# The lower mixture layer of a perceiver block: factor gather spread over the token steps, in eight half tiles

## What is computed

```python
def kmoe(x_flat, W_router, A, B, scale, bias, d_in1, d_in2, d_out1, d_out2, top_k):
    logits = x_flat @ W_router.T
    vals, idx = jax.lax.top_k(logits, top_k)          # 2 of 64 experts
    probs = jax.nn.softmax(vals, axis=-1)
    xs = x_flat.reshape(-1, d_in1, d_in2)
    Y = jnp.einsum('nkoi,nij,nkpj->nkop', A[idx], xs, B[idx])
    out = jnp.einsum('nkop,nk->nop', Y, probs).reshape(-1, d_out1 * d_out2)
    return out * scale + bias
```

## Time and profile before

| | us |
|---|---|
| median of 3 runs | 1326.34 (1323.18 to 1327.03) |
| profiled execution, time | 1326.24 |
| profiled execution, span of its trace | 1324.2 |
| TensorE busy (matmul) | 1235.5, 93% |
| VectorE busy | 809.8, 61% |
| ScalarE busy | 439.6, 33% |
| GpSimd busy | 227.7, 17% |

### The profile page before, as it was taken

One profiled execution on the slowest core, in us unless ns is written; L12 is line 12 of the kernel. 1 busy time (PEld: TensorE's weight loads), 2 busy tenths in 40 slices (PEclk: granted clock), 3 DMA queues, 4 the chain that ended last, 5 costly groups with the idle time before them and its releaser, 6 DMA issues.

```text
span 1324.2 us, 61286 instructions
## 1 busy us (share of the span) xinstructions
PE 1235.5 (93%) x27823; PEld 799.4 (60%) x27823; DVE 809.8 (61%) x1523; ACT 439.6 (33%) x866; POOL 227.7 (17%) x373
## 2 busy tenths in 40 slices
PE   9999999999999999999999998887889888889885
PEld 6764333333333334677666775666777776779775
DVE  5567767776777671455565555555674846465766
ACT  2223211321132112221222211235464646454564
...
DMA packets 68176, 211.50 MB, mean 160 GB/s; under 512 B 14544, under 2 KB 30928, under 8 KB 53616
## 3 DMA queue, kind: packets, MB, share of 16 engines
...
...
## 4 chain that ended last, share of the span: by engine, by line
PE 77%; DVE 10%; issue 5%; DMA 3%; POOL 2%; ACT 2%; SPq 1%; DVEq 0%; POOLq 0%; ACTq 0%
PE ps L715 14%; PE ps L564 10%; PE ps L1088 8%; PE ps L2192 6%; PE ps L2143 4%; PE ps L235 4%; PE ps L1202 4%; PE ps L1109 4%; DVE arena L576 4%; PE ps L479 3%; PE ps L2121 2%; PE ps L2234 2%; PE ps L705 2%; DVE arena L1872 2%; PE ps L2178 2%
## 5 line engine op out<-in xcount | busy, mean ns | idle before, releaser
L576 DVE STREAM_TRANSPOSE arena<-arena 128x448 f32<-128x448 f32 (+1 forms) x512 | 264.0, 578 | 100.8 <-PE ps L564 83.8
L564 PE MATMUL ps<-arena 32*64 32x400 f32 (+1 forms) x4096 | 202.7, 506 | 0.8
L715 PE MATMUL ps<-arena 128*64 128x512 f32 x832 | 189.1, 598 | 0.0
L564 PEld LDWEIGHTS ps<-arena 32*64 32x64 f32 x4096 | 75.3, 130 | 97.2 <-issue 50.7
L715 PEld LDWEIGHTS ps<-arena 128*64 128x64 f32 x832 | 55.5, 136 | 121.3 <-issue 111.9
L599 ACT ACTIVATE arena<-ps,arena 128x384 f32<-128x384 f32 x64 | 36.3, 582 | 276.4 <-DVE arena L590 276.4
L1088 PE MATMUL ps<-arena 128*128 128x256 f32 x512 | 115.1, 383 | 0.8 <-ACT arena L1023 0.8
L1088 PEld LDWEIGHTS ps<-arena 128*128 128x128 f32 x512 | 97.2, 191 | 17.5 <-issue 3.3
L2042 ACT COPY arena<-ps 128x512 f32<-128x512 f32 x128 | 75.1, 588 | 84.3 <-PE ps L2192 57.8
L1872 DVE SCALAR_TENSOR_TENSOR arena<-ps,arena 128x512 f32<-128x512 f32 x64 | 69.8, 1117 | 38.8 <-PE ps L2178 38.4
L888 POOL TENSOR_TENSOR arena<-arena 128x1024 f32<-128x1024 f32 x8 | 18.9, 2368 | 405.8 <-PE ps L715 405.8
...
## 6 DMA issues: line engine op xcount, KB each, us to landing
...
arena<-x SPq DMA_DIRECT2D x16, 512.0 KB, 4.5
...
x_n<-arena SPq DMA_DIRECT2D x16, 512.0 KB, 3.5
```

Source lines behind the costliest of these rows:

```text
L564: last = pe.matmul(ps[b * SEQ:(b + 1) * SEQ, tb, 0:WIDTH[tb]], qs[p % 2][r, db, b * SEQ:(b + 1) * SEQ], z[r, at % RING, b, 0:WIDTH[tb]], s ...
L576: vec.transpose(z[:, at % RING, :, g * 224:g * 224 + nt * 32].rearrange("p b (j t) -> p b j t", t=32), slots[slot_of(k)][:, :, 0:nt, db * ...
L715: last = pe.matmul(ps[b * SEQ:(b + 1) * SEQ, OB, :], probt[:, j, b * SEQ:(b + 1) * SEQ], slot[:, b, jj, :], start=j == 0, stop=j == TILES - 1)
```

## The change

The lower layer works in eight half tiles of eight steps instead of four tiles. A half tile's factors are gathered in 8 units (2 factors x 4 units), each of 16 matmuls with 128 columns into one pair of banks, which ScalarE and VectorE evict together, one bank each. The first nine units (`EARLY`) run ahead of the first step, in three bank pairs; after them each step holds one unit, for the half tile after, in banks 6 and 7. GpSimd copies the unit's table slice (`stage_unit`) and, for every four units, the choices (`stage_choices`) to fixed places. TensorE's loop now has four steps: second, unit, first for each. The logits of the last tile run in one piece before the first step. Results are transposed one eighth at a time in the steps of the next half tile, `y_out` applies the scale, and the residual moves to GpSimd in quarters. Inputs of the residual and results move in eight DMAs of 16 rows for each half tile. The halves of the lower tables change from alternating outputs to contiguous ones, and two semaphores of the self attention become one.

The diff, cut; what is left out repeats the old forms of the functions shown, hands names on, and places the work of the last tile's choices at steps 1 to 11:

```diff
-                sp.dma_start(tables["dn"][n][r, :, :], a[dn].rearrange("e (o f) i -> e o f i", f=2)[:, :, k, :])\
+                sp.dma_start(tables["dn"][n][r, :, :], a[dn][:, k * D1 // 2:(k + 1) * D1 // 2, :])\
...
-    y = tables["up_at"].rearrange("p (t r b) -> p t r b", t=2, r=R)
-    x2b, yt = (wr_at[:, u * 4 * D:(u + 1) * 4 * D].rearrange("p (t f) -> p t f", t=2) for u in range(2))
+    y = tables["up_at"].rearrange("p (u r b) -> p u r b", u=2, r=R)
+    x2b, yt = (wr_at[:, u * 4 * D:(u + 1) * 4 * D].rearrange("p (u f) -> p u f", u=2) for u in range(2))
+    router_at = wr_up.rearrange("p c e -> p (c e)")
+    oh_st = router_at[:, 0:2 * P].rearrange("p (q n) -> p q n", q=4)
...
+    tab_at.append(area.at)
     tab_st = [area(4, D1) for _ in range(2)]
+    slots_dn = [t.rearrange("p (o i) -> p o i", o=4) for t in
+                [arena[:, at:at + 2 * P] for at in tab_at] + [router_at[:, 2 * P:4 * P]]]
...
+    def half_of(j):
+        hh, v, g = j // 8, j // 4 % 2, j % 4
+        return hh // 2, slice(64 * (hh % 2), 64 * (hh % 2) + 64), v, g
+    def unit_bank(j):
+        return 2 * (j % 3) if j < EARLY else 6
+    def gathered_dn(j, hf):
+        _, cols, v, g = half_of(j)
+        dst = fac[v].rearrange("p (m n z) -> p m n z", m=2, z=D1)[:, :, cols, 16 * hf + 4 * g:16 * hf + 4 * g + 4]
+        return dst, ps[:, unit_bank(j) + hf, :].rearrange("p (o m n) -> p m n o", o=4, m=2)
+    def choices_of(j):
+        T, cols, v, _ = half_of(j)
+        x = ohx_dn[T][:, v, :, cols]
+        return x if v == 0 else x.rearrange("p (t k) n -> p k t n", k=2)
+    def units_out(e, count):
+        for s in s_ged:
+            e.wait_ge(s, count + UP + AHEAD - 8)
...
+        def rows_of_half(hh):
             for t in range(2):
-                sp.wait_ge(s_res, 2 * T + t + 1)
-                sp.dma_start(out_v[2 * T + t, :, :], x2b[:, t, :]).then_inc(s_end, 16)
-            sp.wait_ge(s_end, 32 * T + 32)
-        def load_x2(T):
-            for t in range(2):
-                sp.dma_start(x2b[:, t, :], x2_d[2 * T + t, :, :]).then_inc(s_x2, 16)
+                for c in range(C):
+                    q, n, p = hh // 2 * 2 + t, 32 * c + 16 * (hh % 2), 32 * c + 16 * t
+                    yield q, slice(n, n + 16), slice(p, p + 16)
+        def store_out(hh):
+            sp.wait_ge(s_res, 4 * hh + 4)
+            for q, tokens, p in rows_of_half(hh):
+                sp.dma_start(out_v[q, tokens, :], x2b[p, hh % 2, :]).then_inc(s_end, 16)
+        def load_x2(hh):
+            if hh >= 2:
+                sp.wait_ge(s_end, 128 * (hh - 1))
+            for q, tokens, p in rows_of_half(hh):
+                sp.dma_start(x2b[p, hh % 2, :], x2_d[q, tokens, :]).then_inc(s_x2[hh % 2], 16)
...
         load_x2(0)
+        load_x2(1)
         for q in range(4):
             load_h(1, q)
-        for T in range(T_N):
-            if T:
-                store_out(T - 1)
-                load_x2(T)
+        for hh in range(2 * T_N):
+            T = hh // 2
             if T + 2 < T_N:
-                for q in range(4):
+                for q in (hh % 2 * 2, hh % 2 * 2 + 1):
                     sp.wait_ge(s_sth, STEPS * T + PIECE * (q + 1) + UP + AHEAD - 2)
                     load_h(T + 2, q)
-        store_out(T_N - 1)
+            if hh:
+                store_out(hh - 1)
+                if hh + 1 < 2 * T_N:
+                    load_x2(hh + 1)
+        store_out(2 * T_N - 1)
+        sp.wait_ge(s_end, 128 * 2 * T_N)
...
+        def stage_b_dn(s):
+            if s % HALF_STEPS == 0:
+                units_out(pool, s + 8)
+            pool.wait_ge(s_s2, UP + s - 1)
+            pool.tensor_copy(two(st_b[s % 2]), dn[1][:, :, s % STEPS, :]).then_inc(s_stb, 1)
+        def stage_unit(j):
+            if j >= EARLY + 4:
+                pool.wait_ge(s_gd, j - 3)
+            _, _, v, g = half_of(j % UNITS)
+            pool.tensor_copy(slots_dn[g], tab_dn[v][:, 4 * g:4 * g + 4, :]).then_inc(s_td, 1)
+        def stage_choices(j):
+            first = j // 4 * 4
+            pool.wait_ge(s_gd, max(first, EARLY))
+            src = choices_of(j % UNITS)
+            for e in range(2):
+                pool.wait_ge(s_ohe["dn"][e], half_of(j % UNITS)[0] + 1 + CREDIT)
+            dst = oh_st if len(src.shape) == 3 else oh_st.rearrange("p (k t) n -> p k t n", k=2)
+            pool.tensor_copy(dst, src).then_inc(s_oc, 4)
+        def residual(hh, part):
+            u = hh % 2
+            pool.wait_ge(s_x2[u], 128 * (hh // 2) + 128)
+            pool.wait_ge(s_yt, 8 * hh + 2 * part + 2)
+            cols = slice(8 * part, 8 * part + 8)
+            into = x2b[:, u, :].rearrange("n (o p) -> n o p", p=D1)[:, :, cols]
+            pool.tensor_tensor(into, yt[:, u, :].rearrange("n (o p) -> n o p", p=D1)[:, :, cols], into, ALU.add)\
+                .then_inc(s_res, 1)
...
+        stage_b_dn(0)
+        stage_b_dn(1)
+        for j in range(EARLY, EARLY + 3):
+            stage_unit(j)
+        stage_choices(EARLY)
+        for s in range(STEPS * T_N):
+            j = s + EARLY
+            if j + 3 <= UNITS:
+                stage_unit(j + 3)
+            if j % 4 == 3 and j < UNITS:
+                stage_choices(j + 1)
+            if s == 5:
+                exponential("dn", T_N - 1)
+            if s + 2 < STEPS * T_N:
+                stage_b_dn(s + 2)
+            if s >= HALF_STEPS and s % 2:
+                residual(s // HALF_STEPS - 1, s % HALF_STEPS // 2)
+        for part in range(4):
+            residual(2 * T_N - 1, part)
...
+        def y_out(s):
+            hh, n = divmod(s, HALF_STEPS)
+            vec.wait_ge(s_s2, UP + s + 1)
+            if hh >= 2 and n == 0:
+                vec.wait_ge(s_yt, 8 * (hh - 1))
+            vec.tensor_scalar(y[:, hh % 2].rearrange("p (t r) b -> p t r b", t=2)[:, :, rows_of(n), :]
+                              .rearrange("p t r b -> p t (r b)"),
+                              ps[:, 4 + s % 2, 0:P].rearrange("p (t x) -> p t x", t=2), scales[:, 1:2], None, ALU.mult)\
+               .then_inc(s_ye, 1)
+        def results_back(hh, k, pieces):
+            u, w = hh % 2, D1 // pieces
+            vec.wait_ge(s_ye, HALF_STEPS * (hh + 1) + UP + AHEAD + 2)
+            if hh >= 2:
+                vec.wait_ge(s_res, 4 * (hh - 1))
+            cols = slice(k * w, k * w + w)
+            vec.transpose(yt[:, u, :].rearrange("n (o p) -> n p o", p=D1)[:, cols, :],
+                          y[:, u].rearrange("q r p -> q p r")[:, cols, :]).then_inc(s_yt, 8 // pieces)
...
+        for j in range(EARLY):
+            if j == 6:
+                one_hot_out(vec, "dn", T_N - 2, 1, 7)
+            gather_out_dn(j)
+        stage_h(0)
+        stage_h(1)
+        parts(T_N, 6)
+        logits(vec, "dn", T_N - 1, 5)
+        stage_h(2)
+        for s in range(STEPS * T_N):
+            if s + 3 < STEPS * T_N:
+                stage_h(s + 3)
+            y_out(s)
+            if s + EARLY < UNITS:
+                gather_out_dn(s + EARLY)
+            if s >= HALF_STEPS:
+                results_back(s // HALF_STEPS - 1, s % HALF_STEPS, 8)
...
+        for k in range(4):
+            results_back(2 * T_N - 1, k, 4)
...
+        def gather_out_dn(j):
+            if j in (0, 4):
+                act.wait_ge((s_sta, s_stb)[j // 4], UP + AHEAD)
+            act.wait_ge(s_gd, j + 1)
+            dst, src = gathered_dn(j, 0)
+            act.copy(dst, src).then_inc(s_ged[0], 1)
+        def stage_a_dn(s):
+            if s % HALF_STEPS == 0:
+                units_out(act, s + 4)
+            act.wait_ge(s_s1, UP + s - 1)
+            act.copy(two(st_a[s % 2]), dn[0][:, :, s % STEPS, :]).then_inc(s_sad, 1)
...
+        mid_out(UP)
+        stage_a_dn(2)
+        for s in range(STEPS * T_N):
+            if s + 1 < STEPS * T_N:
+                mid_out(UP + s + 1)
+            if s + 3 < STEPS * T_N:
+                stage_a_dn(s + 3)
+            if s + EARLY < UNITS:
+                gather_out_dn(s + EARLY)
...
-        def unit_out(v, g, T):
-            done, first = unit_done(v, g, 0)
-            pe.wait_ge(done, T * (len(BY_ACT[v]) if g in BY_ACT[v] else 8 - len(BY_ACT[v])) + first)
+        def unit_early(j):
+            T, cols, v, g = half_of(j)
+            if j >= 3:
+                units_out(pe, j - 2)
+            x = choices_of(j)
+            for o in range(4):
+                for q in range(2):
+                    for hf in range(2):
+                        r = slice(hf * E, (hf + 1) * E)
+                        last = pe.matmul(ps[q * E:(q + 1) * E, unit_bank(j) + hf, o * P:(o + 1) * P],
+                                         tab_dn[v][r, 4 * g + o, :], x[r, 2 * q:2 * q + 2, :] if v == 0 else x[r, q],
+                                         start=True, stop=True)
+            last.then_inc(s_gd, 1)
+        def unit_dn(n, g):
+            pe.wait_ge(s_td, n + 1 + UP + AHEAD)
+            for s in s_ged:
+                pe.wait_ge(s, n + 1 + UP + AHEAD)
+            if g == 0:
```

(91 more changed lines are left out.)

219 lines of the change are left out of this document (66 added, 153 removed).

## The result

The changed kernel takes 1310.14 us (median of 4 runs, 1308.36 to 1311.35) against 1326.13 us of the kernel before on the same chip: ratio 0.9884, interval 0.9867 to 0.9900. It is faster, by 16.0 us. I had predicted 1291 us, 35 us faster, with 1307 as the upper end. The direction was right, the size was more than twice too large, and the time lies outside my range.

What follows compares the result with a forecast made beforehand. TensorE was taken to set the pace, slowed by gather waits, a low clock and the start. From 1106.8 us, terms of 182.5 us ended the span at 1289.3, 34.9 earlier: 1291 us against 1326.3, range 1277 to 1307.

Steps and rivals of the forecast that it cites:

- 1, 2: up to the loop: Before the loop: nine early units with transposes and waits 10.4 us, then logits, two first_dn and fold; 20.6 us in all.
- 3: code the first time: Loop code on its first pass: one stall of 2.02 us as in the old second step; bounds nothing to 8.
- 4: 56 steps: Loop steps with a unit, last a dummy: 56 at 2.36 us plus 14 loop turns at 0.31, 136.5 us.
- 5: transposes: Last tile's choices transposed after 12 steps: 1.25 us, eviction and signal 0.85, restart 0.3; 2.4 us.
- 6: last eight steps: Steps without a unit after the loop: three pairs at 3.21 us, the last two 1.5; 11.1 us.
- 7: the end: After the last matmul: transposes, last residual, eight stores, landing and close; 9.9 us, the same as before.
- Rival B: Clock falls in the long loop for 35 us, steps of 4.26 us, 15 us lost: 1306 us; chance 10%.
- rivals C and F: In the loop: VectorE or GpSimd copies exclude each other, 1302 us, 11%; or every eviction exposed, 1338 us, 2%.
- rival D: In the loop, sequencer runs ahead during units, short passes go faster: 2.1 us a step, about 1275 us; chance 7%.
- Rival E: Loop body refetched on further turns: one 2.02 us stall a turn gives 1317 us, two 1343; chance 3%.
- A to D: Cases counted as faster: the main forecast (1291 us, own range 1283 to 1300, 67%) and the first three rivals.

## Why the prediction was wrong

By its own steps, predicted and measured in the profiled execution:

| step | predicted | measured | of it not foreseen |
|---|---|---|---|
| 1, 2: up to the loop | 20.6 | 25.7 | gaps 3.5, clock 0.88 in the logits |
| 3: code the first time | 2.0 | 6.65 | 4.65 |
| 4: 56 steps | 136.5 | 137.6 | about 3 of low clock; steps and turns 2.7 cheaper than forecast |
| 5: transposes | 2.4 | 2.75 | |
| 6: last eight steps | 11.1 | 17.4 | gap 1.8, clock about 4 |
| 7: the end | 9.9 | 11.2 | 1.3, eight more stores in the queue |
| sum | 182.5 | 201.2 | |

**The step that failed is 3, "Code the first time through: one stall of 2.02 us as in the old second step".** I took one row of a two-step loop as the price of the whole four-step body, and costed no code at all for the early units, the logits and the tail, which also run for the first time. What the runs showed in its place is a rate: 256 instructions in 3.8 us, so 1.3 us for each step of new code beyond the first, and up to 4.2 beside full data queues. My upper bound for the step, 8 us, held (6.65 in the first turn); but the first turn was one stretch of three, and in steps 1, 2 and 6 there were 5.3 us more of gaps. In all 12 us of gaps stood where I had 2. The old row misled for a reason that its neighbours show: the kernel before met nearly as much new code in this part (8 packets on the instruction queue from 1107 to 1175 us, 10 here from 1105), but 128 passes of its gather, of 256 columns each, a block's worth, took 7.1 us (144 in 8.00), well over 3.8. The new logits need 3.7 for as many (169 in 4.87), a step of the loop 2.33. So the old gather could hide its code and the new passes can't; this is argued from the rows, no run tests it by itself.

**What follows from the gaps** I had not costed either: the clock. It stood at 0.88 in the logits, fell for a unit or two behind the longest gap and behind the transposes, and was at its low level for six of the last eight steps. In the kernel with its tail inside the lap loop these eight took 13.0 us at full clock with a gap of 1.25, so 11.8 without it; of the 17.4 us here 1.8 are then the gap and about 4 the clock. Rival B had the clock falling, but in the loop and for 35 us; it fell elsewhere, behind gaps. That a gap brings it down is supported by the kernel with the unit under a branch and contradicted by one kernel, so it is the likely cause of these 4 us and not a shown one.

**Step 7** missed that `results_back` of the seventh half ends with step 63, so that its eight stores queue directly ahead of the last eight. Of the 7.5 us of issues 1.5 were on the path, as the profiles of the kernels with early results showed.

**What was right.** Step 4: unit, evictions, staging and results as the sum had them, 2.33 us a step against 2.36, with no wait for VectorE or GpSimd (rivals C and F), not 2.1 as in rival D, and no instruction packet from 1175.0 to 1277.9 us. That its total agrees to 1% is partly luck: 56 steps of 2.33 and 14 turns of 0.24 are 133.8 us, and low clock behind the first turn's longest gap and behind the transposes filled the difference. The slack for GpSimd's choices was real but thin: the kernel with the second factor in front lost it, 1.1 us each time. Rival E was rightly judged unlikely for this body, by the old kernel's 1,280 instructions that stayed; at eight steps it came, at 19.3 us a turn. In the list of rivals two figures are off and change nothing: some 47 and not 44 steps with a unit have transposes beside them (C would be 1303), and A to D with half of E make 0.965 and not 0.95. The small DMAs of x2 and results were hidden but for the end. The loads of the second tile's activations and of x2, hidden as data, were not free: they lengthened the gaps of the first turn by 2.2 us.

**What stays open.** Why the clock held in one kernel behind the same gap. And the gap among the early units, 1.95 us here and 1.95 to 2.8 in the kernels of the experiments. That it is code too is argued from its place: 127 passes and as many weight loads lie between it and the next gap, close to the 256 instructions that lie between the gaps of the loop.
